# Key norms of a delta-rule attention layer from ScalarE's accumulator sums, with masks, a fed tile and the closing sums in other places of the order

## The reference

```
x = x + attention(layernorm(x));  x = x + ffn(layernorm(x))
attention: q, k, v = silu(causal conv over 4 tokens of (x W)), 4 heads of 64
           q, k divided by their norm over each head's 64 values
           beta = sigmoid(x Wb);  Kb = k beta, Vb = v beta
           in chunks of 64 tokens: A = Kb k^T (all heads summed)
           T = inverse of (1 + strictly lower part of A);  W = T Kb, U = T Vb
           scan over chunks:  u = U - W * diag(S);  o = q diag(S) + tril(q k) u;  S += k^T u
           o normalised per head by its mean square, times g, times Wo
ffn:       2 shared experts for all tokens; 8 routed experts, the best 2 for each token,
           weighted by a softmax of their two scores; each is gelu(x W1) W2, width 1024
```

## Time and profile before

| | |
|---|---|
| median of 3 runs | 1232.56 us (1231.97 to 1234.34) |
| the profiled execution, its own time | 1232.95 us |
| its span, first to last instruction | 1231.2 us |
| PE busy | 1114.2 us, 90% |
| DVE busy | 694.7 us, 56% |
| ACT busy | 622.5 us, 51% |
| POOL busy | 365.0 us, 30% |
| mean granted clock of PE | 0.962 of full speed |

### The profile page before, as it was taken

How to read it: one execution, slowest core, us unless ns; L and a number is a source line. 1 busy time by engine, 2 the same in 40 slices (tenths; PEclk the granted TensorE clock), 3 DMA queues, 4 the chain that set the end, 5 groups by cost and what they waited for, 6 DMA issues and landing times.

```text
span 1231.2 us, 25608 instructions
## 1 busy us (share of the span) xinstructions
PE 1114.2 (90%) x9320; PEld 959.5 (78%) x9321; DVE 694.7 (56%) x1211; ACT 622.5 (51%) x1117; POOL 365.0 (30%) x320
## 2 busy tenths in 40 slices
PE   4596889999999998877988989999999999999996
PEld 1464768787878787766877878898999998999996
DVE  4667857676767675575689642333333333333377
ACT  4565556756565655355633643444444444444442
POOL 0415343424252425122011112334334334333100
PEclk9698879999999999998999989999999999999998
DMA  3202020202020102253222421111111111111456
GB/s 131 69 18 69 1 77 1 78 10 78 10 78 10 61 10 95 78 156 112 95 86 78 138 61 57 43 50 52 43 51 49 45 51 47 47 51 51 145 197 230
DMA packets 54088, 86.36 MB, mean 70 GB/s; under 512 B 6656, under 2 KB 39296, under 8 KB 53888
## 3 DMA queue, kind: packets, MB, share of 16 engines
q1 hardware_dynamic: 46336, 64.37, 16.2%
q0 software_dynamic: 7680, 20.98, 5.5%
HBM read 60.16 MB, written 25.17 MB: 69 GB/s over the span
## 4 chain that ended last, share of the span: by engine, by line
PE 65%; DVE 11%; issue 11%; ACT 6%; POOL 5%; DMA 2%; SPq 0%; DVEq 0%; ACTq 0%; POOLq 0%
PE ps L1398 25%; PE ps L1378 22%; PE ps L1232 4%; PE ps L1389 3%; PE ps L1222 2%; PE ps L1297 2%; POOL W L823 2%; PE ps L1456 2%; POOL W L842 2%; PE ps L1304 1%; ACT W L1071 1%; DVE late_room L1749 1%; PE ps L1358 1%; DVE W L1560 1%; DVE W L1652 1%
## 5 line engine op out<-in xcount | busy, mean ns | idle before, releaser
L1378 PE MATMUL ps<-late_room,W 128*128 128x256 f16 x3072 | 352.9, 273 | 28.5 <-DVE late_room L1749 22.6
L1398 PE MATMUL ps<-W,late_room 128*128 (+1 forms) x3264 | 373.2, 274 | 0.3 <-DVE late_room L1749 0.3
L1378 PEld LDWEIGHTS ps<-late_room,W 128*128 (+1 forms) x3072 | 298.6, 98 | 70.4 <-DVE late_room L1749 28.5
L1398 PEld LDWEIGHTS ps<-W,late_room 128*128 128x128 f16 x3264 | 321.7, 99 | 40.4 <-DVE late_room L1749 0.5
L1097 ACT ACTIVATE ps<-ps 128x512 f32<-128x512 f32 x272 | 158.6, 583 | 354.5 <-PE ps L1378 316.8
L1749 DVE SCALAR_TENSOR_TENSOR late_room<-ps,late_room 128x512 f16<-128x512 f32 x272 | 181.0, 687 | 233.4 <-ACT late_room L1102 233.4
L1102 ACT ACTIVATE late_room<-ps 128x512 f16<-128x512 f32 x272 | 155.7, 595 | 2.5
L1560 DVE SCALAR_TENSOR_TENSOR W<-W 128x512 f32<-128x512 f32 x144 | 109.1, 758 | 10.2 <-ACT W L959 6.8
L940 ACT COPY W<-ps 128x512 f32<-128x512 f32 x112 | 61.5, 589 | 86.7 <-PE ps L1297 70.4
L1232 PE MATMUL ps<-W 128*128 128x512 f16 x384 | 97.3, 399 | 7.1 <-DVE W L1575 3.8
L1997 DVE TENSOR_SCALAR late_room<-ps 128x512 f32<-128x512 f32 x36 | 24.9, 691 | 97.7 <-PE ps L1398 97.7
(11 more groups left out here) (188 smaller groups left out, 1372.1 us busy)
## 6 DMA issues: line engine op xcount, KB each, us to landing
wstage<-in_w_ffn SPq DMA_DIRECT2D x40, 512.0 KB, 3.8
W<-yt_d SPq DMA_DIRECT2D x16, 512.0 KB, 5.8
late_room<-in_x SPq DMA_DIRECT2D x8, 512.0 KB, 4.6
W<-in_x SPq DMA_DIRECT2D x8, 512.0 KB, 4.1
x2n_d<-W SPq DMA_DIRECT2D x8, 512.0 KB, 3.1
base_d<-W SPq DMA_DIRECT2D x8, 512.0 KB, 3.6
late_room<-base_d SPq DMA_DIRECT2D x16, 256.0 KB, 4.2
acc_d<-late_room SPq DMA_DIRECT2D x12, 256.0 KB, 2.2
```

The lines of the kernel that those rows point to most:

```text
L1378: last = pe.matmul(up_bank(n, c)[:, f * XT:(f + 1) * XT], weight(slot, d, hw, cols), x_halves[:, hx, d], start=(q == 0), stop=(q == len(pa ...
L1398: last = pe.matmul(down_bank(b)[:, c * D:(c + 1) * D], hs[b][:, hh, f, c * P:(c + 1) * P], weight(slot, DB + f // 4, hw, cols), start=(q = ...
```

## The change

1. The key squares and their sums: ACT no longer squares after silu. PE turns the keys out right after the last projection, ACT squares them from PSUM in 16 instructions of 64 columns (4 token blocks by 4 heads), each with `accum_out`, POOL powers 8 columns twice. PE's eight matmuls, the PSUM bank `ssq` and ACT's copy are gone. `project(1)` goes ahead of the turned keys.
2. The first level waits for the first mask and no longer for all five. A is kept in `KbT`'s room in place of `Y`'s.
3. In the tail DVE's scan moves from slot 2 to slot 3, behind the level-2 addition; the query norms are taken up in slot 6 of the next tick; POOL's power for the output norm moves from slot 6 to slot 5.
4. The splits of the shared weights move to slots 12 and 13 of ticks 1 to 3.
5. The last fed tile: its up parts move from slots 8 to 15 of tick 10 to slots 2, 3 and 8 to 11, in other banks; its first two down parts to slots 12 and 14 of tick 10, the other two to slot 1 of tick 11. The fed tile before has two down parts in slot 1.
6. At the end each unit's kept sums are combined ahead of its `y_shared`, and the last tile's routed outputs are added to its base (`ahead`) at u = 5, so nothing but the last `y_shared` and a store is left behind the last down part.

```diff
 FRONT_FILLS = (
-    [(f"proj{m}", "act") for m in PROJ_ORDER[:7]]
-    + [("ssq", "act")]
+    [(f"proj{m}", "act") for m in PROJ_ORDER]
     + [(f"tokK{h}", "dve") for h in range(2)]
-    + [(f"proj{PROJ_ORDER[7]}", "act")]
...
+DOWN_SLOTS_TAIL = {1: ((0, 0), (0, 1)), 5: ((1, 0),), 6: ((1, 1),)}
+Y_SLOTS = {3: 0, 6: 1}
+UP_SLOTS_TAIL = {2: ((0, 0), (0, 1)), 3: ((0, 2), (0, 3)), 8: ((1, 0),), 9: ((1, 1),), 10: ((1, 2),), 11: ((1, 3),)}
+DOWN_SLOTS_LAST = {1: ((1, 0), (1, 1))}
+DOWNS_AHEAD = {12: (0, 0), 14: (0, 1)}
...
+SUMS_AT = {2: [("acc", 0), ("acc", 1), ("final", 0)], 3: [("acc", 2), ("acc", 3)], 4: [("acc", 4), ("acc", 5), ("final", 1)],
+           5: [("acc", 6), ("acc", 7), ("ahead", 3)], 6: [("acc", 8), ("acc", 9), ("final", 2)], 7: [("acc", 10), ("acc", 11)]}
...
-SPLIT_AT = [(8, 1), (9, 1), (13, 1), (14, 1), (8, 2), (9, 2), (13, 2), (14, 2)]
+SPLIT_AT = [(12, 1), (12, 1), (13, 1), (12, 2), (12, 2), (13, 2), (12, 3), (13, 3)]
...
                 if slot == 5:
-
-                    pool.wait_ge(*fr.empty(n, "ssq"))
-                    pool.tensor_tensor(ssq, ssq, minus_half[:, 0:GT * NH], ALU.pow).then_inc(rnorm, 1)
+                    for h in range(2):
+                        part = ssq[:, 2 * NH * h:2 * NH * (h + 1)]
+                        pool.wait_ge(squares, 4 * NH * n + 2 * NH * (h + 1))
+                        pool.tensor_tensor(part, part, minus_half[:, 0:2 * NH], ALU.pow).then_inc(rnorm, 1)
...
-                    if m in (2, 3):
-                        act.wait_ge(silu_done, 3 * DB * n + i + 1)
-                        act.activation(sqK[:, m - DB], at, ACT.Square).then_inc(squares, 1)
...
+                def key_squares(h):
+
+                    act.wait_ge(*fr.full(n, f"tokK{h}"))
+                    if n:
+
+                        act.wait_ge(masked, (LEVELS - 1) * n)
+                    for g in range(2 * NH):
+                        act.activation(sqK[:, h, g * HD:(g + 1) * HD], fr.bank(f"tokK{h}")[:, g * HD:(g + 1) * HD], ACT.Square,
+                                       accum_out=ssq[:, 2 * NH * h + g:2 * NH * h + g + 1]).then_inc(squares, 1)
...
                 if slot == 5:
-                    act.wait_ge(*fr.full(n, "ssq"))
-                    act.copy(ssq, fr.bank("ssq")[:, 0:GT * NH]).then_inc(fr.empty(n, "ssq")[0], 1)
+                    project(1)
+                    for h in range(2):
+                        key_squares(h)
                     silu(4)
...
-                    pe.wait_ge(squares, DB * (n + 1))
-                    head_sums(fill(fr, n, "ssq"), sqK).then_inc(fr.sem_full, 1)
                 if slot == 5:
-                    turn_out(fr, n, "tokK0", Kr, 0)
-                if slot == 6:
-                    turn_out(fr, n, "tokK1", Kr, 1)
                     project(1)
+                    pe.wait_ge(silu_done, 3 * DB * n + DB)
+                    for h in range(2):
+                        turn_out(fr, n, f"tokK{h}", Kr, h)
...
                     if slot % 2 == 0:
+                        pe.wait_ge(masked, (LEVELS - 1) * n + s)
                         if s == 1:
-
-                            pe.wait_ge(masked, (LEVELS - 1) * (n + 1))
...
                                       prod.rearrange("p a d (c t) -> p (a d c) t", t=CH), AX_X, ALU.add).then_inc(chunk_sums, 1)
+                if slot == 3:
+
                     dve.wait_ge(chunk_sums, n + 1)
...
-                    y_shared(final_tile(v), e)
...
+                    for s in SUMS_AT.get(u, ()):
+                        if s[0] == "acc":
+                            combine(s)
+                    if u == N_SH * (FINAL - 1):
+
+                        dve.wait_ge(combined, XB * TOPK * (SUMS.index(("ahead", FINAL - 1)) + 1))
                     y_shared(final_tile(v), e)
```

More of the change, by code:

```diff
@@ L272 @@
 assert G_ROUTED % 2 == 0 and R_TILES % 2 == 0
-SUM_UNITS = range(2, N_SH * FINAL + 1)
-PER_SUM = G_ROUTED // (len(SUM_UNITS) - 1)
-assert PER_SUM * (len(SUM_UNITS) - 1) == G_ROUTED
-def sums_at(u):
-    own = [("final", u // N_SH - 1)] if u % N_SH == 0 else []
-    kept = range(PER_SUM * (u - 2), min(PER_SUM * (u - 1), G_ROUTED))
-    return own + [("acc", q) for q in kept]
-SUMS = [s for u in SUM_UNITS for s in sums_at(u)]
+SUMS_AT = {2: [("acc", 0), ("acc", 1), ("final", 0)], 3: [("acc", 2), ("acc", 3)], 4: [("acc", 4), ("acc", 5), ("final", 1)],
+           5: [("acc", 6), ("acc", 7), ("ahead", 3)], 6: [("acc", 8), ("acc", 9), ("final", 2)], 7: [("acc", 10), ("acc", 11)]}
+SUM_UNITS = range(2, N_SH * FINAL)
+SUMS = [s for u in SUM_UNITS for s in SUMS_AT[u]]
+assert FINAL == 4 and G_ROUTED == 12 and len(SUMS) == FINAL + G_ROUTED
 def sum_rows(s):
@@ L787, in _ @@
             for u in SUM_UNITS:
-                for s in sums_at(u):
-                    store_sums(s)
+                for s in SUMS_AT[u]:
+                    if s[0] != "ahead":
+                        store_sums(s)
                 if u + 2 in SUM_UNITS:
@@ L1105, in up_piece @@
             def up_piece(slot, n, b):
-                if slot >= UP_SLOT:
-                    e, c = divmod(slot - UP_SLOT, 4)
+                for e, c in ups(slot, n):
                     u = N_SH * n + e
@@ L1400, in down_part, with down_fed @@
                 return last
+            def down_fed(n, e, c):
+                if c == 0:
+                    pe.wait_ge(h_low, 4 * N_SH * n + 4 * (e + 1) if n == FED - 1 else 4 * N_SH * n + 4 + 3 + e)
+                    if n == FED - 1:
+                        pe.wait_ge(y_out, N_SH * (n - 1) + e + 1)
+                last = down_part(e, c, e)
+                if c == XB - 1:
+                    last.then_inc(down_done, 1)
             def up_piece(slot, n, b):
-                if slot >= UP_SLOT:
-                    e, c = divmod(slot - UP_SLOT, 4)
+                if n == FED - 1 and slot in DOWNS_AHEAD:
+                    down_fed(n, *DOWNS_AHEAD[slot])
+                for e, c in ups(slot, n):
                     u = N_SH * n + e
-                    if slot == UP_SLOT:
+                    if (e, c) == (0, 0):
                         if not n:
@@ L1419, in down_piece @@
             def down_piece(slot, n, b):
-                if slot in DOWN_SLOTS:
-                    e, c = DOWN_SLOTS[slot]
-                    if c == 0:
-                        pe.wait_ge(h_low, 4 * N_SH * n + 4 + 3 + e)
-                    last = down_part(e, c, e)
-                    if c == XB - 1:
-                        last.then_inc(down_done, 1)
+                for e, c in downs(slot, n):
+                    down_fed(n, e, c)
             def rank_rows():
@@ L1450, in turn @@
                 pe.wait_ge(*x_there(t))
+                if isinstance(t.g, int) and not t.turn:
+                    pe.wait_ge(*tl.empty(GROUPS - 1, "logits"))
                 if not isinstance(t.g, int) or t.turn:
@@ L1596, in front, with flat, back @@
                     dve.tensor_tensor(XTr, XTr, idt[:].unsqueeze(1).to_broadcast([P, GT, P]), ALU.add).then_inc(x0t_ready, 1)
-                if slot == 14:
+            def flat(a):
+                return a.rearrange("p k t -> p (k t)")
+            def back(slot, n, b):
+                if slot == 6:
                     dve.wait_ge(enorm, n + 1)
@@ L1600, in front @@
                     dve.tensor_tensor(edge(QT[b], b), edge(QT[b], b), rn, ALU.mult).then_inc(q_edges, 1)
-            def flat(a):
-                return a.rearrange("p k t -> p (k t)")
-            def back(slot, n, b):
                 if slot < 10 and slot % 2:
@@ L1769, in up_piece @@
             def up_piece(slot, n, b):
-                if slot >= UP_SLOT:
-                    e, c = divmod(slot - UP_SLOT, 4)
+                for e, c in ups(slot, n):
                     low(N_SH * n + e, e, c)
             def down_piece(slot, n, b):
-                if slot in DOWN_SLOTS and DOWN_SLOTS[slot][1] == XB - 1:
-                    y_shared(fed_tile(n), DOWN_SLOTS[slot][0])
+                if slot in Y_SLOTS:
+                    y_shared(fed_tile(n), Y_SLOTS[slot])
             def split_piece(slot, t):
@@ L1959, in combine @@
                     sums = acc[v]
+                elif kind == "ahead":
+                    dve.wait_ge(base_in[final_tile(v).par], 16 * final_tile(v).shared())
+                    sums = bt[final_tile(v).par]
                 else:
```

53 lines of the change are left out of this document (34 added, 19 removed).

## The result

The changed kernel takes 1237.84 us in the median of 8 runs (1236.08 to 1242.35), the kernel before 1232.26 in 8 runs: 1.0047 times as long, with a 95% interval of 1.0033 to 1.0062. The profiled execution of it took 1242.35 us (span 1240.5), 4.5 above its own median, so differences of a microsecond or two between single places of two traces are read with care. Where two traces have the same code in the ticks, both are used: the second experiment has the changed kernel's up to tick 9, and the first has that of the kernel before.

A forecast was written before the change was run, and what follows sets the result against it. PE was taken to bound the kernel, with DVE and ACT close behind. Terms for ticks 1 to 11, the early tile and the end summed to +2.4 us on 1232.95, giving 1235.3; likeliest 1230 to 1240, whole range 1220 to 1247.

The forecast's parts named there:

- The price of a square: ACT's time for one 64-column square with accumulator output: taken as 0.33 us, 16 making 5.3 us a group.
- the rival of cheap squares: Squares cost up to 0.22 us, so PE's own order bounds Z: 1222 us, 1220 at 0.18; chance 0.28.
- The slope: How square time reaches the total: 16 squares a group, counted in about 7.2 of the 8 groups.
- The scan behind the addition: In full ticks DVE's scan ends 3.1 us late; PE waits 1.7 us for ACT's reading, then 0.6 for a bank.
- A full tick: Ticks 5 to 8: Z begins 2.7 us later in each, +10.8 us over the four.
- The forecast's own floor: In full ticks, squares cheaper than 0.22 us gain no more, as PE's own order then bounds Z.
- Ticks 1 to 4: First ticks, with earlier masks and moved splits: -1.9 us in tick 1, -1.7 in ticks 2 and 3, +1.0 in tick 4.
- POOL's output power: Moving it a slot earlier in the tail costs nothing, as POOL is busy for 30% of the span.
- Tick 9: No front: Y's 3.84 us wait for the addition goes, the later scan's output is paid: -2.1 us.
- Ticks 10 and 11: Output sums come 4.2 us later; PE reaches the early tile 4 us early and waits for DVE: +0.7 us.
- The rival of a falling clock: New gaps ahead of PE in full ticks halve matmul speed behind them: +10 us, 1245 us; chance 0.07.
- The end: Kept sums combined ahead of the last down part, so the store is issued earlier: -4.4 us, give or take 1.

The follow-up runs named there:

- the second experiment: The changed kernel with the last fed tile back in its old slots: 1234.75 us, 1.0016 times the kernel before.
- the first: The kernel before with only the new order of the end's sums: 1225.01 us, 0.9943 times the kernel before.
- the ninth experiment: The changed kernel with 11 more squares in each group, 27 in place of 16: 1256.33 us, 1.0190 times the kernel before.
- fifth run: The changed kernel with only DVE's scan back in slot 2, POOL's output power left in slot 5: 1228.27 us, 0.9961 times the kernel before.
- seventh run: The kernel before plus key squares on ACT, masks level by level, POOL's output power and query norms moved, and the end's sums: 1221.13 us, 0.9899 times.
- eighth run: The seventh run's kernel with the splits moved to slots 12 and 13: 1220.67 us, 0.9918 times the kernel before.
- third: The changed kernel with the scan, POOL's output power and the query norms back in their old places: 1254.23 us, 1.0179 times the kernel before.
- fourth: The changed kernel with the key norms' old path and one wait for all five masks: 1273.47 us, 1.0341 times the kernel before.
- sixth: The fourth run's kernel with POOL's output power back in slot 6: 1248.70 us, 1.0129 times the kernel before.

## Why the prediction came out right, and which of its steps did not

The forecast was 1235.3, slower; the measurement says 1237.84, slower. Of a change of 5.6 us the forecast had about half, and even that is luck: the squares were priced far too dear, and about as much was missing elsewhere, in ticks 1 to 4, in tick 9 and ahead of the early tile. The base was off by a little as well. The change of +2.4 was added to the profiled execution's 1232.95, which stood 0.39 above the median; from the median it gives 1235.0, the edge of what the forecast itself called no change (1230.1 to 1235.0).

- **The price of a square: wrong.** I took 0.33 from the nearest row with an operand per partition; it is 0.196, next to the low end of 0.18 that the two small instructions 0.14 apart gave. By the ninth experiment that error is worth about 18 us. The Trainium skill's figures (ScalarE: Activation LUTs, What ACT_TABLE_LOAD costs) would have given 0.146, nearer than my choice and too low by 0.05. At the true price the rival of cheap squares should have come, at 1220 to 1222. It did not, so terms of about the same size were missing.
- **The slope was right.** I said that 0.9 of what is added to the squares is on the path; the ninth run shows about all of it.
- **The scan behind the addition: right mechanism, too small a part of the sum.** Its wait on PE was forecast at 1.7 us and is 1.66, the one for the bank at 0.6 and is 0.83. But I let the dear squares hide behind it in one sum of 2.7 a tick. Apart from each other (fifth run) the scan costs 1.8 to 2.1 us in a full tick and 9.6 us in the whole kernel, and the squares give back 0.5 a tick.
- **A full tick: +2.7 forecast**, +1.5 found in ticks 7 and 8. The forecast's own floor, for squares of 0.22 or less, is 2.7 - 16 x 0.11 = +0.9. The four full ticks make +6.0 (264.4 in the second run, 258.5 in the first, both at a clock of 1.00), where +10.8 was forecast. The floor was right about what bounds Z: ACT idles 0.48 us ahead of the copies.
- **Ticks 1 to 4: wrong.** -2.6 forecast; +4.3 and -1.3 found in the two traces with this code, against the one trace of the kernel before, and +6.2 and +0.7 against the first run, which has the same ticks. Tick 1 gave 4.0 to 4.6 where I forecast 1.9. Ticks 2 to 4 lost more than that. Part of that is the late splits. The forecast had named their wait for the third piece, but booked it at 1.5 in tick 1; it lands behind the start of tick 2. ACT waits 4.38 us for the piece's transfer, with its copy of the first level behind it, and PE's Z waits for that (changed kernel, then seventh run):

```profile
60.15 1.06 ACT L1141 ACTIVATE W<-wstage 128x1024 f16<-128x1024 f32 x1 [4.38 <-DMA wstage<-in_w_ffn]
61.73 2.08 PE L1323 MATMUL ps<-W 128*128 128x128 f32 x8 [4.27 <-ACT W L955]
```

```profile
58.69 1.16 PE L1307 MATMUL ps<-W 128*128 128x128 f32 x8 [1.78 <-ACT W L938]
```

  In tick 3 that Z waits 3.43 us, and in the seventh run not at all. The eighth run puts the splits at 3 to 4 us. These ticks also have no down part behind the turned keys, so squares, silu and copies lie open, and the fourth Z waits 2.80, 2.80 and 2.14 us for ACT:

```profile
84.06 1.36 PE L1323 MATMUL ps<-W 128*128 128x128 f32 x8 [2.80 <-ACT W L955]
...
137.49 1.13 PE L1323 MATMUL ps<-W 128*128 128x128 f32 x8 [2.80 <-ACT W L955]
...
197.41 2.00 PE L1323 MATMUL ps<-W 128*128 128x128 f32 x8 [2.14 <-ACT W L955]
```

  I had these ticks bounded by POOL's masks and never costed that wait. But it is little more than the key sums that it stands for (1.92 us and up to 0.66 of wait): the seventh run has it too, at 2.81, 2.81 and 2.80, and its ticks 2 to 4 take 166.5 us, where the kernel before takes 166.3 and the first run 164.1.
- **POOL's output power: its "nothing" had a wrong reason, though no term of the sum shows it.** I excused the move by POOL's low busy share. In truth it is the condition of the whole change: without it (and the query norms' place) the squares cost 26 us more (third against fifth run), and with the old norms it costs 25 us (fourth against sixth). Whether such an edit costs nothing is read from the entries ahead of it and behind it in its queue, not from how busy the queue is.
- **Tick 9: wrong.** -2.1 forecast, +0.4 found in both traces with this code. The Y that had waited 3.84 us now waits 0.83, as forecast. The late scan's output costs 1.46 us ahead of Z and 0.26 ahead of the sums, which is what the forecast had left for it (3.84 - 2.1). What it had not is the clock: from 514.2 to 521.0 it is at 0.55, and sums and down part take 2.96 and 5.06 us, 1.84 and 2.78 at the higher level. That is 3.4 us more, where the kernel before lost some 1.8 in this tick behind its wait of 3.84:

```profile
514.20 2.96 PE L1244 MATMUL ps<-W 128*128 128x2 f32 x16 [0.26 <-DVE W L1733]
517.02 5.06 PE L1417 MATMUL ps<-W,late_room 128*128 128x256 f16 x24
```

- **Ticks 10 and 11: right mechanism, wrong size.** The sums were forecast 4.2 late and are 4.3 late; PE arrives early and waits for DVE, as said. It gets to the early tile 1.7 later where +0.7 was forecast, and the idle of 7.28 us ahead of it brings down the clock for 1.9 us more, which I had at nothing. The fed tile is the cause: undone it gives 3.1 us, and 7.6 with the scan early.
- **The rival of a falling clock: dismissed too easily.** I held against it that PE is at work on both sides of each gap. Tick 7 bears that out, but tick 6 of the changed kernel loses 1.7 us behind its gap of 2.13, tick 9 is slowed in both traces, and in the third and sixth runs full ticks are slowed behind 2.43, and 1.66 and 1.84. It did not come as a whole (three to four full ticks of the changed kernel), but it is part of what was missing.
- **The end: right.** -4.4 forecast, -4.9 in the trace, -6.9 (-4.2 to -9.9) in the first run. The store is issued 1.7 us behind the last matmul, where 2.3 was forecast.

What stays open: why the masks, worth 4.3 us at the start of tick 2, are worth only 1 to 3 in the seventh kernel; why the late splits, 3 to 4 us in the ticks' traces, do not show in the eighth run's median; and what decides whether the clock falls behind a gap of some 2 us. The query norms' new place was never tested alone.

## What to carry to other kernels

An in-order queue with a third of its time busy can still be the bound: list for each wait what stands behind it in the queue, and who needs that. When one producer of a shared engine becomes later, the order of all its customers there has to be looked at again (here 25 us, over four times what the whole change moved). A wait ahead of PE can cost more than its length, by the clock behind it, so both are read from the rows. Bound an unknown price by rows of instructions of the same size first, and state what the answer would be at that end before choosing another row.
